# A gated attention and mixture-of-experts kernel: expert bias on TensorE, residual ahead of the experts, a reordered drain and tail

## The reference

```python
x = x + tanh(g_xattn) * cross_attention(layernorm(x), ctx)      # 16 heads of 16, 4 key heads
h0 = layernorm(x)
h = h0 + attention(layernorm(h0, ln1))                          # 16 heads of 128, rotary, causal, biases
z = layernorm(h, ln2)
raw = softmax(z @ w_gate)                                       # 4 experts
vals, idx = top_k(raw, 2); w = softmax(vals)                    # the two weights of a token
comb = zeros.at[idx].add(w)
hmid = gelu(z @ we1[e] + be1[e])                                # erf Gelu, 256 wide
m = sum over e of comb[:, e] * (hmid[e] @ we2[e] + be2[e])
x = x + tanh(g_ffn) * (h + m)
```

## Time and profile before

| | us |
|---|---|
| median of three runs | 479.84 (479.81 to 480.1) |
| profiled execution, span from first to last instruction | 478.2 |
| PE busy in the span | 415.9 (87%) |
| DVE busy | 386.1 (81%) |
| POOL busy | 283.2 (59%) |
| ACT busy | 272.7 (57%) |
| mean granted PE clock | 0.984 |

### The profile page before, as it was taken

One profiled execution on the slowest core, in us unless ns is written; L12 is line 12 of the kernel. 1 busy time (PEld: TensorE's weight loads), 2 busy tenths in 40 slices (PEclk: granted clock), 3 DMA queues, 4 the chain that ended last, 5 costly groups with the idle time before them and its releaser, 6 DMA issues.

```text
span 478.2 us, 10292 instructions
## 1 busy us (share of the span) xinstructions
PE 415.9 (87%) x3150; PEld 361.7 (76%) x3150; DVE 386.1 (81%) x1190; ACT 272.7 (57%) x614; POOL 283.2 (59%) x383
## 2 busy tenths in 40 slices
PE   0189998889867799999999999999999996588994
PEld 0168876677645699899899899899898986467894
DVE  4876769786977888888798797898898767876997
ACT  2027655545122767766867677587677677265440
POOL 5946718902437858767677587587687544153541
PEclk9999999989999999999999999999999998979999
DMA  8200000200225677595685775865865663100011
GB/s 284 49 1 3 2 1 3 88 2 1 46 45 117 142 166 133 110 217 115 132 203 109 159 162 108 203 137 112 193 132 108 147 89 66 46 0 2 0 46 44
DMA packets 71347, 44.53 MB, mean 93 GB/s; under 512 B 57360, under 2 KB 59536, under 8 KB 71312
## 3 DMA queue, kind: packets, MB, share of 16 engines
q1 hardware_dynamic: 67392, 35.42, 34.8%
q10 hardware_dynamic: 3920, 8.69, 6.5%
HBM read 13.68 MB, written 1.05 MB: 31 GB/s over the span
## 4 chain that ended last, share of the span: by engine, by line
PE 64%; DVE 23%; issue 5%; POOL 4%; DMA 3%; ACT 1%; SPq 0%; ACTq 0%; DVEq 0%; POOLq 0%
PE bank L1229 34%; PE bank L1297 5%; PE bank L1343 5%; DVE yacc L1084 3%; PE bank L1344 2%; PE bank L1296 2%; DVE yacc L1093 2%; PE bank L1169 2%; PE bank L1210 2%; DVE nxm L858 2%; PE bank L1126 1%; DVE qk_room L887 1%; PE bank L1170 1%; DMA rows_sb<-in_rows 1%; DVE room L887 1%
## 5 line engine op out<-in xcount | busy, mean ns | idle before, releaser
L428 POOL TENSOR_TENSOR room<-room,qk_room 128x512 f32<-128x512 f32 x64 | 82.2, 1285 | 41.5 <-DMA qk_room<-qk_room 40.8
L594 ACT ACTIVATE probs<-sm,nm 128x128 f32<-128x128 f32 (+1 forms) x128 | 56.9, 446 | 49.3 <-DVE nm L970 49.2
L586 ACT ACTIVATE probs<-turned 128x768 uint16<-128x768 uint16 x64 | 69.0, 1078 | 17.8 <-DMA turned<-halves 16.4
L1229 PE MATMUL bank<-hH,qk_parts 128*128 128x512 f32 x240 | 75.5, 395 | 0.0
L440 POOL COPY halves<-probs 128x768 uint16<-128x768 uint16 x64 | 52.6, 822 | 35.8 <-DVE probs L1016 35.8
L887 DVE SCALAR_TENSOR_TENSOR qk_room<-bank,qk_bias,cst_sb 128x512 f32<-128x512 f32 x64 | 48.0, 749 | 29.9 <-PE bank L1229 27.8
L1229 PE MATMUL bank<-hL,qk_parts 128*128 128x512 f32 x120 | 58.0, 483 | 6.0 <-POOL qk_parts L374 3.0
L1229 PEld LDWEIGHTS bank<-hH,qk_parts 128*128 128x128 f32 x240 | 45.2, 188 | 9.6
L1229 PE MATMUL bank<-woH,o_parts 128*128 128x256 f32 x256 | 48.0, 285 | 0.0
L887 DVE SCALAR_TENSOR_TENSOR room<-bank,qk_bias,cst_sb 128x512 f32<-128x512 f32 x64 | 47.4, 741 | 0.0
L1229 PE MATMUL bank<-woL,o_parts 128*128 128x256 f32 x128 | 39.3, 307 | 8.1 <-DVE yacc L1007 2.5
(11 more groups left out here) (211 smaller groups left out, 1230.0 us busy)
## 6 DMA issues: line engine op xcount, KB each, us to landing
qk_room<-qk_room SPq DMA_DIRECT2D x128, 128.0 KB, 2.4
stg<-in_wqkv ACTq DMA_DIRECT2D x6, 768.0 KB, 5.6
stge<-in_we ACTq DMA_DIRECT2D x7, 256.0 KB, 3.1
stg<-in_wqkv SPq DMA_DIRECT2D x2, 768.0 KB, 6.3
stgo<-in_wo ACTq DMA_DIRECT2D x6, 256.0 KB, 3.4
x_sb<-in_x SPq DMA_DIRECT2D x4, 256.0 KB, 6.0
turned<-halves SPq DMA_TRANSPOSE x64, 2.8
out_y<-yacc SPq DMA_DIRECT2D x4, 256.0 KB, 2.1
```

Of the source, the lines that this page charges most:

```text
L428: pool.tensor_tensor(v, v, qk_sw[:, q, :], ALU.subtract).then_inc(s["rope_done"], 1)
L586: act.activation(PTs[:, 1 - q, 0:384].bitcast(U16).rearrange("p (n h) -> p h n", h=2), turned[:, (j - 3) % 4, :, :].rearrange("p (h c) n - ...
L594: ins = act.activation(PR[:, q, a:e], sm[:, q, a:e], ACT.Exp, bias=nm[:, q, t:t + 1], scale=-1.0, accum_out=rs[:, q, t:t + 1])
L1229: ins = pe.matmul(outp, l, r, start=(m == 0), stop=(m == n - 1))
```

## The change

- **Bias.** be2 is loaded twice (4 KB each, rows 0 and 32 of a buffer) by SP at the start, in place of the spread 512 KB copy late. POOL builds two tiles right after its first `low_o`: `be2_parts`, zero but for the high part in row 0 and the low part in row 32, and `both_rows`, zero but for ones in these rows. In `expert_out` one more matmul, both_rows x be2_parts, opens each bank half. The 32 DVE steps of L1084 go. A new semaphore, be2_ready, is waited for by SP ahead of the first transpose and by PE ahead of expert 0.
- **Residual.** yacc x tanh(g_ffn) + x is formed ahead of the gate's chain, on whole batches; the gate's last factors are scaled by tanh(g_ffn) in its place. SP writes a batch out on c_acc.
- **Banks.** Three sets of output banks for the experts. The last three output products use banks 5, 7, 5; turn 3 uses bank 5.
- **Gate.** The second softmax (of two values) is formed by Tanh, 0.5 -+ 0.5 tanh(d/2), in place of Exp, sum, reciprocal; ACT runs the first Exp ahead of Gelu 6 and the Tanh ahead of Gelu 8.
- **Order.** In the drain (T from 58 on) ACT takes probabilities ahead of the merge, DVE the maxima one unit ahead and `o_low` ahead of the sum; the second layernorm's phases move. In the tail PE's order is middles 2 and 3, turns 2 and 3, expert 0, middle 4, logits, middle 5, gate transposes, expert 1, then from middle 6 on as before. POOL's and ACT's parts of batches 2 and 3 move from ahead of middles 2 and 4 to ahead of middles 4 and 5.

The diff, cut to its core:

```diff
-            return bank[5 if isinstance(m, int) and m == NU // 2 - 1 else 7]
+            return bank[5 if isinstance(m, int) and m >= NU // 2 - 3 and m % 2 else 7]
+
+        def late(i, j):
+
+            return isinstance(i, int) and U * i + j >= NU - LEAD
+
+        def turn_bank(b):
+
+            return bank[5 if b == B - 1 else 4]
...
         def out_bank(m, hf):
 
-            return bank[(6, 2)[m % 2] + hf]
+            return bank[(2, 6, 4)[m % 3] + hf]
...
+            for row in (0, 32):
+                sp.dma_start(be2_in[row:row + 1, :, :], be2.rearrange("(o e) n -> o e n", o=1)).then_inc(s["d_be"], 16)
...
                 if unit(i, j, 1):
                     sp.wait_ge(s["b_split"], U * i + j)
+                    if i == 0 and j == 1:
+                        sp.wait_ge(s["be2_ready"], 1)
...
             unrolled_steps(step)
-            sp.wait_ge(s["wqk_ready"], 4 * NP)
-            sp.wait_ge(s["wv_ready"], NP)
-            sp.dma_start(be2_rows, be2.rearrange("(o e) n -> o e n", o=1).to_broadcast([P, E, D])).then_inc(s["d_be"], 16)
             for b in range(B):
-                sp.wait_ge(s["c_fin"], b + 1)
+                sp.wait_ge(s["c_acc"], 2 * E * (b // 2 + 1) - 1 + b % 2)
                 sp.dma_start(out_v[:, 2 * b:2 * b + 2, :], yacc[:, 2 * b:2 * b + 2, :]).then_inc(s["d_out"], 16)
...
             pool.tensor_copy(woH[:, :, :], stgo[:, :, :]).then_inc(s["wo_half"], 1)
             low_o(0)
+
+            pool.memset(be2_parts[:, :, :].bitcast(F32), 0.0).then_inc(s["be2_zero"], 1)
+            pool.memset(both_rows[:, :].bitcast(F32), 0.0).then_inc(s["be2_zero"], 1)
+            pool.wait_ge(s["be2_zero"], 2)
+            pool.wait_ge(s["d_be"], 32)
+            for row in (0, 32):
+                one = slice(row, row + 1)
+                pool.memset(both_rows[one, :].bitcast(F32), 1.0).then_inc(s["be2_zero"], 1)
+                pool.tensor_copy(be2_parts[one, :, :], be2_in[one, :, :]).then_inc(s["be2_high"], 1)
+            pool.wait_ge(s["be2_high"], 2)
+            pool.wait_ge(s["be2_zero"], 4)
+            low = slice(32, 33)
+            pool.tensor_tensor(be2_parts[low, :, :], be2_in[low, :, :], be2_parts[low, :, :].bitcast(F32), ALU.subtract).then_inc(s["be2_ready"], 1)
...
             for n in range(2 * NE):
-                if n in (2, 4):
-                    hidden_low2(1 + n // 2)
+                if n in (4, 5):
+                    hidden_low2(n - 2)
...
-                    if unit(i, j, 2):
-                        act.wait_ge(s["b_split"], T - 1)
-                    for t in range(2):
-                        a, e = ((0, P), (P, 3 * P))[t]
-                        ins = act.activation(PR[:, q, a:e], sm[:, q, a:e], ACT.Exp, bias=nm[:, q, t:t + 1], scale=-1.0,
-                                             accum_out=rs[:, q, t:t + 1])
-                        ins.then_inc(s["b_exp"], 1)
+                    probabilities(i, j)
...
             act.wait_ge(s["b_wo"], NU // 2)
             for n in range(2 * NE):
-                if n in (2, 4):
-                    hidden_high2(1 + n // 2)
-                if n == 4:
-
+                if n in (4, 5):
+                    hidden_high2(n - 2)
+                if n == 6:
                     act.wait_ge(s["c_gmax"], 1)
                     act.activation(gate[:, 64:96], gate[:, 32:64], ACT.Exp).then_inc(s["c_gexp"], 1)
+                if n == 8:
+
                     act.wait_ge(s["c_gdiff"], 1)
-                    act.activation(gate[:, 400:408], gate[:, 392:400], ACT.Exp).then_inc(s["c_gexp"], 1)
+                    act.activation(gate[:, 400:408], gate[:, 392:400], ACT.Tanh, scale=-0.5).then_inc(s["c_gexp"], 1)
                 c, m = divmod(n, NE)
...
-            while_exp = {63: [(0, 0)], 64: [(0, 1), (0, 2)], 65: [(0, 3)]}
-            extra = {65: [(0, 4), (0, 5)],
-                     66: [(1, 0), (1, 1)], 67: [(0, -1), (1, 2), (1, 3), (1, 4), (1, 5)], 68: [(1, -1)]}
+            extra = {63: [(0, 0), (0, 1)], 64: [(0, 2), (0, 3), (0, 4), (0, 5)], 65: [(1, 0), (1, 1), (1, 2)],
+                     66: [(1, 3), (1, 4), (1, 5), (0, -1)], 67: [(1, -1)]}
 
             def step(i, j):
                 T = U * i + j
                 q = j % 2
-                if unit(i, j, 0) and not (isinstance(i, int) and T == 0):
+                if unit(i, j, 0) and not (isinstance(i, int) and (T == 0 or T > NU - LEAD)):
                     maxima(i, j)
+                if late(i, j) and T < NU - 1:
+                    maxima(*divmod(T + 1, U))
...
-                last = isinstance(i, int) and i == NP
-                if unit(i, j, 4) and last:
+                if unit(i, j, 4) and late(i, j):
                     o_low(i, j)
-                if last:
-                    for b, phase in extra.get(T, []):
-                        second_t(b) if phase < 0 else second_norm(b, phase)
...
-                if unit(i, j, 4) and not last:
+                if unit(i, j, 4) and not late(i, j):
                     o_low(i, j)
-                for b, phase in extra.get(T, []) if isinstance(i, int) and not last else []:
+                for b, phase in extra.get(T, []) if isinstance(i, int) else []:
                     second_t(b) if phase < 0 else second_norm(b, phase)
...
+            half_g, minus_half_g = small[:, 140:141], small[:, 141:142]
+            dve.tensor_scalar(half_g, small[:, 97:98], 0.5, None, ALU.mult)
+            dve.tensor_scalar(minus_half_g, small[:, 97:98], -0.5, None, ALU.mult)
+            for b in range(B):
+                y = yacc[:, 2 * b:2 * b + 2, :].rearrange("p t n -> p (t n)")
+                xb = x_sb[:, 2 * b:2 * b + 2, :].rearrange("p t n -> p (t n)")
+                dve.scalar_tensor_tensor(y, y, small[:, 97:98], xb, ALU.mult, ALU.add).then_inc(s["c_base"], 1)
...
             dve.wait_ge(s["c_gexp"], 2)
-            link(dve.tensor_scalar(Gt(248, 8), Gt(400, 8), 1.0, None, ALU.add))
-            link(dve.reciprocal(Gt(256, 8), Gt(248, 8)))
-            link(dve.tensor_tensor(Gt(264, 8), Gt(256, 8), Gt(400, 8), ALU.mult))
+            dve.tensor_scalar(Gt(256, 8), Gt(400, 8), half_g, half_g, ALU.mult, ALU.add)
+            link(dve.tensor_scalar(Gt(264, 8), Gt(400, 8), minus_half_g, half_g, ALU.mult, ALU.add))
             dve.tensor_tensor(V3(120), V3(120), Gt(256, 8).unsqueeze(2).to_broadcast([P, NT, E]), ALU.mult)
             link(dve.tensor_tensor(V3(152), V3(152), Gt(264, 8).unsqueeze(2).to_broadcast([P, NT, E]), ALU.mult))
             link(dve.tensor_tensor(Gt(0, 32), Gt(120, 32), Gt(152, 32), ALU.add))
-            dve.wait_ge(s["d_be"], 16)
-            dve.wait_ge(s["b_yadd"], NU // 2)
+            dve.wait_ge(s["c_base"], B)
...
             for m in range(2 * E):
 
                 c, e = divmod(m, E)
                 for hf in range(2):
                     b = 2 * c + hf
+                    dve.wait_ge(s["c_exp_pe"], 2 * m + hf + 1)
                     if m:
                         dve.wait_ge(s["c_acc"], 2 * (m - 1) + hf + 1)
-                    for t in range(2):
-                        n = 2 * b + t
-                        ins = dve.scalar_tensor_tensor(yacc[:, n, :], be2_rows[:, e, :], gate[:, 4 * n + e:4 * n + e + 1], yacc[:, n, :],
-                                                       ALU.mult, ALU.add)
-                    ins.then_inc(s["c_be"], 1)
-                for hf in range(2):
-                    b = 2 * c + hf
-                    dve.wait_ge(s["c_exp_pe"], 2 * m + hf + 1)
...
                     for t in range(2):
                         n = 2 * b + t
                         ins = dve.scalar_tensor_tensor(yacc[:, n, :], out_bank(m, hf)[:, 256 * t:256 * (t + 1)],
                                                        gate[:, 4 * n + e:4 * n + e + 1], yacc[:, n, :], ALU.mult, ALU.add)
                     ins.then_inc(s["c_acc"], 1)
-                    if e == E - 1:
-                        dve.wait_ge(s["c_acc"], 2 * m + hf + 1)
-                        y = yacc[:, 2 * b:2 * b + 2, :].rearrange("p t n -> p (t n)")
-                        xb = x_sb[:, 2 * b:2 * b + 2, :].rearrange("p t n -> p (t n)")
-                        dve.scalar_tensor_tensor(y, y, small[:, 97:98], xb, ALU.mult, ALU.add).then_inc(s["c_fin"], 1)
 
...
-                if b:
+                if 0 < b < B - 1:
                     pe.wait_ge(s["c_hT"], b)
+                if b == B - 1:
+                    pe.wait_ge(s["b_yadd"], NU // 2)
...
             def expert_out(m):
                 c, e = divmod(m, E)
                 pe.wait_ge(s["c_gL"], 2 * m + 2)
-                if m < 2:
+                if m == 0:
+                    pe.wait_ge(s["b_oL"], NU)
+                    pe.wait_ge(s["be2_ready"], 1)
+                if m == 1:
                     pe.wait_ge(s["b_yadd"], NU // 2)
+                if m == 2:
+                    pe.wait_ge(s["c_gmax"], 1)
                 for hf in range(2):
-                    if m >= 2:
```

(23 more changed lines are left out.)

53 lines of the change are left out of this document (34 added, 19 removed).

## The result

The changed kernel takes 487.65 us (482.84 to 488.29, four executions) against 479.82 for the kernel before, a ratio of 1.0138 (1.0105 to 1.0171). Measured once more, six executions beside thirteen, it is 485.45 against 481.20: 1.0118 (1.0075 to 1.0161). The direction was as forecast, the size was not: +7.8 and +4.3 us, where +1.4 stood and the range ended at +3.2. The profiled execution has a span of 486.0 us at a mean granted clock of 0.971 (before: 478.2 at 0.984).

What follows compares the result with a forecast made beforehand. In the tail DVE and PE were both taken as nearly full, so relieving DVE wins little before PE is full. Tail in sum -1.0 plus head +2.4 gave +1.4: span 479.6, time 481.2 us, range 477.8 to 483.0.

Steps and rivals of the forecast that it cites:

- Head, +2.4: Attention part: POOL's 6.1 us block holds DVE's small steps, so PE waits; +2.4 us, bounds 0 and +3.3.
- one stretch more or less: PE's slow-clock stretches, expected in the tail too: one more or less is worth at most 1.7 us.
- Drain, +0.5: Drain's new order: POOL's L383 0.7 us later at worst, DVE's work the same; +0.5 us, bounds -2 and +1.2.
- Tail, PE's stream, +0.4: Tail: bias product adds 3.76 us on PE, stalls go; PE ends 0.4 us later, 1.7 if half the stalls stay.
- The +1.0 for holds: Gate chain and second layernorm: POOL holds DVE's small steps; +1.0 us, bounds 0 and +2.5; gate chain with holds 12.5.
- Rival B: Tail: the gate chain becomes the bound, each hold past the room costing 1.3 us; 482.5 us, chance 0.13.
- Behind PE, -2.9: After PE's last matmul: 6.3 us fall to 3.4, as DVE keeps only a pair of sums; gain 2.9 us.
- my doubt: Gate: Tanh might need two more table loads ahead of Gelu 8; about 1 us if the gate chain is late, else nothing.
- A: Head: POOL's block is harmless, only the tail's -1.0 stands; 478.8 us, 477.1 with drain's and clock's gain; chance 0.26.
- C: Head costs as forecast, but the drain's reorder gains 2 us or a clock stretch comes back; 478.9 to 479.5, chance 0.20.
- The last line: Prediction's closing risk: wrong above all if POOL's block is short, or if PE's slow stretches move; no size given.

Runs made afterwards that it cites:

- the first and second run: Changed kernel with POOL's block moved behind the second batch: 482.67 us (1.0036); kernel before plus SP's two loads, POOL's block and SP's wait alone: 483.52 us (1.0074).

## Why the prediction was wrong, step by step

- **Head, +2.4: right in mechanism and hold, too small in what follows.** Block 6.1 us forecast, 6.2 measured; its subtraction 2.4 and 2.34; L858 at 99.7 forecast, 99.95 measured; PE resumes 2.3 us later. Mis-sized is the clock term: I let it stand in the bound ("+3.3 with a longer slow-clock stretch") and took nothing for it. What follows the hold came to 1.6 us in the first profiled execution, so +3.9, and to 1.0 in the second, so +3.3.
- **Slow clock elsewhere: a term that the sum didn't have.** I had priced one stretch more or less at 1.7 us and put it into the drain and a rival alone. The ramp's stretch at 168 us cost 1.5 in the first profiled execution, the one at 147 nothing. The runs do not tie it to the change: the second profiled execution lost nothing there, and the run without the block lost 2.5. The same idle time in the kernel before was followed by full clock; what else decides is not shown by these runs. That it varies from execution to execution is shown by the change's own four: 482.84 at clock 0.982, three near 487.9 at 0.971.
- **Drain, +0.5 with +1.2 as the worse bound: the step that failed.** Measured +4.4 and +2.8 in the change's two traces and +3.9 by the run of the drain alone. I wrote that L383 would come "0.7 us later at worst" and that DVE has "the same work as before in another order". The order was the cost: the normalisation of each late unit, and the sum, stand behind a low part that waits for ACT's output copy, and the new order of ACT puts the merge (1.06 us) between the probabilities and that copy. I followed L383 back to the probabilities and not to the low part in front of the normalisation. Of the 4.4 us, 1.5 are L383's delay, 2.2 arise from there to the first sum, which waits behind the next low part, and 0.7 from there to the last; the longer slow clock is some 0.5 of it by the two traces.
- **Tail, PE's stream, +0.4: right.** 44.3 us from the first expert forecast, 45.0 measured; the product's price 3.76 and 3.65; no stall left in the window. The +1.0 for holds was not needed: the gate's chain was held (9.6 us against 6.1; 12.5 had been the bound) and still fitted into the room of three bank sets. Rival B did not occur.
- **Behind PE, -2.9: right.** 3.5 us forecast 3.4, against 6.3 before, -2.8.
- **Tanh: my doubt was idle.** The rows of the changed kernel show a load for Exp (446.54) and one for Gelu (448.09), and none at the Tanh (452.87) or the Gelu after it. Where the Trainium skill's "ScalarE: Activation LUTs", section "Table sets: the hidden batching unit", names Tanh with Exp's set, this trace shows it also runs after Gelu without a load.
- **Rivals.** A (head harmless) falls with the first and second run. C's "drain's reorder works" is the opposite of what happened; with the low part behind the normalisation the new order is level with the old one (477.74 and 478.00), so no gain over it can be told even then.
- **Range.** The worst bounds that the prediction names (PE's stream +1.7, holds +2.5, drain +1.2, with -2.9 behind PE) add to +2.5 for the tail, where the range took +1.5; with the head's +3.3 they come to +5.8, and the range ended at +3.2. The last line named the risk: wrong "if PE's slow stretches move".

In us of the first profiled execution: forecast 2.4 + 0.5 + 1.4 - 2.9 = +1.4; measured 3.9 + 1.5 (ramp) + 4.4 + 0.8 - 2.8 = +7.8.

## What to carry to other kernels

When steps of an in-order engine change places, follow back, for each step that now stands behind another, what that other waits for, and on its engine too what was moved ahead of it; "same work, other order" is no price. Put set-up work of POOL where DVE has no short steps on SBUF, whatever number of partitions it touches. And where PE's chain is idle for some us, a further delay can cost twice, itself and the clock afterwards (2.3 us and 1.0 to 1.6 in the head here), so give the clock a term of its own and not only a place in the range. Last, profile a kernel twice before its time is split by stages: here two executions of one kernel differed by 3.9 us, in three stages.
